# A graph, attention and expert layer on one core: pairs of heads in the order keys, values, queries, with other placements of the products that stand around them

## The reference

```
xn = layernorm(x)                                   # x: 1250 x 1024, 40000 edges (src, dst)
h  = relu(gcn(relu(batchnorm(gcn(xn + pe, W1, b1))), W2, b2))
       # gcn: normalised adjacency (deg**-0.5 on both sides, self loops) times x @ W
q, k, v = xn @ Wq, xn @ Wk, xn @ Wv                 # 16 heads of 64
q_, k_  = relu(q @ proj), relu(k @ proj)            # 256 features a head
attn = (q_ @ (k_.T @ v)) / (q_ @ k_.sum(0) + eps)
x  = x + h + attn @ Wo + bo
x  = x + experts(layernorm(x))                      # top 2 of 8, gated
```

## Time and profile before

| | |
|---|---|
| median of three runs | 1712.08 us (1710.87 to 1712.32) |
| the profiled execution | 1707.89 us |
| its span, first to last instruction | 1705.8 us |
| TensorE matmul busy | 1512.8 us, 89% |
| TensorE weight load busy | 1422.9 us, 83% |
| DVE busy | 803.6 us, 47% |
| ACT busy | 526.4 us, 31% |
| chain that ended last, by engine | PE 76%, DVE 7%, ACT 7%, DMA 5% |
| mean granted TensorE clock | 0.956 of full speed |

### The profile page before, as it was taken

The page is one execution under the profiler, slowest core; times in us unless marked ns, Lnnn a source line. Parts: engine busy times, 40 slices in busy tenths (PEclk is TensorE's granted clock), DMA queues, the critical chain, the costliest instruction groups (busy, mean ns, idle before and its releaser), DMA issues.

```text
span 1705.8 us, 21129 instructions
## 1 busy us (share of the span) xinstructions
PE 1512.8 (89%) x8316; PEld 1422.9 (83%) x8316; DVE 803.6 (47%) x1588; ACT 526.4 (31%) x595; POOL 153.3 (9%) x162
## 2 busy tenths in 40 slices
PE   1689999999999999889899899998997549999996
PEld 1679888989898989789899899998997548998885
DVE  4555565555555564542446333344234455554430
ACT  3324243333334243323222133311111214454441
POOL 0010010101010102000000000000000012222321
PEclk9799999999999999999899999999999559999998
DMA  9531231322121313539344023320442926766763
GB/s 283 181 51 27 39 70 27 73 54 46 51 48 49 51 49 69 208 148 231 101 130 109 13 62 106 100 61 30 114 116 58 304 70 192 199 177 192 188 154 74
DMA packets 72744, 183.62 MB, mean 108 GB/s; under 512 B 8987, under 2 KB 39823, under 8 KB 70927
## 3 DMA queue, kind: packets, MB, share of 16 engines
q1 hardware_dynamic: 52550, 135.17, 25.3%
q0 software_dynamic: 20096, 47.10, 14.9%
HBM read 124.15 MB, written 67.93 MB: 113 GB/s over the span
## 4 chain that ended last, share of the span: by engine, by line
PE 76%; DVE 7%; ACT 7%; DMA 5%; issue 3%; SPq 1%; POOL 0%; POOLq 0%; DVEq 0%; ACTq 0%
PE slot L1441 34%; PE slot L1498 11%; PE slot L1671 6%; PE slot L1681 6%; PE slot L1585 3%; PE kvb L1671 3%; PE kvb L1553 2%; PE slot L1539 2%; DMA raw<-adj_d 2%; PE slot L1576 2%; DMA adj_d<-stage 1%; SPq L500 1%; PE slot L1654 1%; PE lsb L1424 1%; PE lsb L1647 1%
## 5 line engine op out<-in xcount | busy, mean ns | idle before, releaser
L1441 PE MATMUL slot<-big_hi,slab_h 128*128 128x418 f32 x1152 | 294.7, 364 | 26.2 <-issue 8.8
L1441 PE MATMUL slot<-big_lo,slab_h 128*128 128x418 f32 x1152 | 286.6, 357 | 0.0
L1441 PE MATMUL slot<-big_hi,slab_l 128*128 128x418 f32 x1152 | 283.6, 354 | 0.0
L1441 PEld LDWEIGHTS slot<-big_hi,slab_h 128*128 128x128 f32 x1152 | 213.1, 191 | 36.2 <-issue 15.1
L1441 PEld LDWEIGHTS slot<-big_lo,slab_h 128*128 128x128 f32 x1152 | 219.8, 191 | 3.4
L1441 PEld LDWEIGHTS slot<-big_hi,slab_l 128*128 128x128 f32 x1152 | 219.4, 191 | 3.6
L684 POOL DMA_DIRECT2D adj_d<-stage x80 | 67.6, 845 | 585.0 <-ACT stage L752 347.0
L1498 PE MATMUL slot<-adj,xs_h 125*128 125x418 f32 x480 | 118.1, 354 | 0.8 <-DVE ztmp L963 0.5
L1498 PE MATMUL slot<-adj,xs_l 125*128 125x418 f32 x480 | 117.4, 353 | 0.0
L718 POOL DMA_INDIRECT xg<-flat_d,token x32 | 31.3, 977 | 775.2 <-DVE token L1375 657.8
L1498 PEld LDWEIGHTS slot<-adj,xs_h 125*128 125x128 f32 x480 | 90.5, 189 | 2.3 <-DVE ztmp L963 0.7
(11 more groups left out here) (266 smaller groups left out, 2470.8 us busy)
## 6 DMA issues: line engine op xcount, KB each, us to landing
slab_raw<-slabs_dram SPq DMA_DIRECT2D x48, 512.0 KB, 3.8
ws_raw<-w_dram SPq DMA_DIRECT2D x36, 512.0 KB, 5.9
adj_d<-stage POOLq DMA_DIRECT2D x81, 117.2 KB, 3.1
w_raw<-w_dram SPq DMA_DIRECT2D x9, 1024.0 KB, 4.9
adj_d<-eye_dram POOLq DMA_DIRECT2D x1, 6250.0 KB, 26.7
raw<-adj_d SPq DMA_DIRECT2D x3, 1828.8 KB
mix_d<-mixt SPq DMA_DIRECT2D x8, 627.0 KB, 5.0
mix_in<-mix_d SPq DMA_DIRECT2D x8, 627.0 KB, 4.2
```

The costliest lines, as they stand in the source:

```text
L1441: mm = ten.matmul(ps[:, 512 * q:512 * q + CW], w[a][:, kt, :], big[b][:, kt, CW * q:CW * q + CW], start=(kt == 0 and c == 0), stop=(kt == ...
```

## The change

The order of a pair's slabs becomes K, V, Q. The copy of Q's result out of PSUM is a key of its own, `QE`, behind `KK 2`. `KK 0` moves behind the whole Q product, and even `KK` tiles go to `lsb` while odd ones go to the slot whose turn it is, without using up the turn (`places_of`), so Q's slot stays taken until `QE`. `VT` now stands behind `AT p 1` and ahead of `RC` and Q. The ten groups of a pair stand six inside K (behind blocks 2 to 7) and four inside V (behind 3, 4, 6, 7); none is left between the QP products. In `AT p 1` DVE writes `nrm` while ACT writes `num`. In the last pair both heads' QP products come ahead of both AT products, with a second buffer `qp_end`. `RH` moves from behind `KK 5` to behind `KK 6`. At the start, `LN`, `LNS`, `LNB` and `XT` of the tiles are interleaved, `BASE` goes behind the first batch, `WR` behind `XT 7`; the identity copy waits for the first slab. `DG` moves from ahead of `O 5` to ahead of `O 6`; `DT` transposes the degree sums themselves, and their inverse roots are made for each node apart (ACT root, Newton step).

```diff
@@ -54,7 +54,7 @@
-        s += [("K", p), ("Q", p), ("V", p)]
+        s += [("K", p), ("V", p), ("Q", p)]
@@ -68,7 +68,7 @@
-        share[("K", p)], share[("Q", p)] = 6, 4
+        share[("K", p)], share[("V", p)] = 6, 4
@@ -80,7 +80,7 @@
-PARTS = {0: (), 2: (5, 7), 4: (1, 3, 5, 7), 6: (2, 3, 5, 6)}
+PARTS = {0: (), 2: (5, 7), 4: (3, 4, 6, 7), 6: (2, 3, 4, 5, 6, 7)}
@@ -89,39 +89,33 @@
-        inside = WITHIN[key][:4]
-        o += [("EO", g) for g in inside] + [("E", g) for g in inside] + then + [key]
-        return o + [("EO", g) for g in WITHIN[key][4:] if key[0] == "K"]
-
-    o = [("BASE",), ("WR",)]
-    for n, (a, b) in enumerate(LN_TILES):
-        o += [("LN", i) for i in range(a, b)] + [("LNS", n)] + [("LNB", i) for i in range(a, b)]
-        if n:
-            o += [("XT", i) for i in range(*LN_TILES[n - 1])]
-    o += [("XT", NT - 2), ("P", 0), ("XT", NT - 1), ("MP",), ("BASE2",)]
+        return o + [("EO", g) for g in WITHIN[key]] + [("E", g) for g in WITHIN[key]] + then + [key]
+
+    ln = lambda *tiles: [("LN", i) for i in tiles]
+    o = ln(0, 1) + [("LNS", 0), ("BASE",), ("LNB", 0), ("LNB", 1)] + ln(2, 3, 4) + [("LNS", 1), ("LNB", 2)]
+    o += ln(5, 6) + [("XT", 0), ("LNB", 3), ("XT", 1)] + ln(7) + [("LNS", 2), ("LNB", 4), ("XT", 2), ("LNB", 5)]
+    o += ln(8) + [("XT", 3), ("LNB", 6)] + ln(9) + [("LNS", 3), ("LNB", 7), ("XT", 4), ("LNB", 8), ("XT", 5)]
+    o += [("LNB", 9), ("XT", 6), ("XT", 7), ("WR",), ("P", 0), ("XT", 8), ("XT", 9), ("MP",), ("BASE2",)]
...
-        o += ([("KK", p, 0)] if p == 0 else []) + [("KK", p, 1), ("KK", p, 2)]
+        o += [("KK", p, 0), ("KK", p, 1), ("KK", p, 2), ("QE", p)]
         for i in range(3, NT):
             o += [("KV", p, i - 3), ("KK", p, i)]
-            if p and i == 5:
+            if p and i == 6:
                 o.append(("RH", p - 1))
...
-        o += with_split(("K", p + 1)) if more else []
-        behind = WITHIN[("K", p + 1)][4:] if more else []
-        o += [("AT", p, 0), ("QP", p, 1, 0)] + [("EP", g) for g in behind[:1]] + [("E", g) for g in behind[:1]]
-        o += [("QP", p, 1, 1)] + [("EP", g) for g in behind[1:]] + [("E", g) for g in behind[1:]]
-        o += with_split(("Q", p + 1)) if more else []
-        o += [("AT", p, 1), ("RC", p)]
-        o += with_split(("V", p + 1)) + [("KK", p + 1, 0), ("VT", p + 1)] if more else [("RH", p)]
+        if not more:
+            o += [("QP", p, 1, 0), ("QP", p, 1, 1), ("AT", p, 0), ("AT", p, 1), ("RC", p), ("RH", p)]
+            continue
+        o += with_split(("K", p + 1))
+        o += [("AT", p, 0), ("QP", p, 1, 0), ("QP", p, 1, 1)] + with_split(("V", p + 1))
+        o += [("AT", p, 1), ("VT", p + 1), ("RC", p)] + with_split(("Q", p + 1))
     for f in range(KD):
-        if f == 5:
-            o.append(("DG",))
         if f == KD - 1:
             o += [("DT",), ("ZP", 1, 0)]
-        o += with_split(("O", f), {3: [("RP", 0), ("RP", 1)], 4: [("RP", 2)]}.get(f, []))
+        o += with_split(("O", f), {3: [("RP", 0), ("RP", 1)], 4: [("RP", 2)], 6: [("DG",)]}.get(f, []))
...
+def places_of():
+
+    place, before, last, turn = {}, {}, {}, 0
+    for k in ORDER:
+        if k[0] not in PSUM_KINDS:
+            continue
+        if k[0] == "KK":
+            place[k] = (2, turn)[k[2] % 2]
+        else:
+            place[k] = turn
+            turn = 1 - turn
+        before[k] = last.get(place[k])
+        last[place[k]] = k
+    return place, before
...
-            pool.wait_ge(x_landed[NT - 1], LAND)
+            pool.wait_ge(slab_landed[0], 16)
...
-                    copy(chunks(num[o:o + 64, :]), cols(ps)[a:a + 64])
-                    ins = copy(chunks(nrm[o:o + 64, :]), cols(ps)[b:b + 64], bias=ATT_EPS)
-                    ins.then_inc(act_done, 1)
+                    if h == 0:
+                        copy(chunks(nrm[o:o + 64, :]), cols(ps)[b:b + 64], bias=ATT_EPS)
+                    copy(chunks(num[o:o + 64, :]), cols(ps)[a:a + 64]).then_inc(act_done, 1)
...
+                elif kind == "AT":
+                    if k[2] == 1:
+                        dve.wait_ge(psum_full, u)
+                        if k[1]:
+                            dve.wait_ge(att_stored, 32 * k[1])
+                        ts(chunks(nrm[64:128, :]), cols(ps)[0:64], ATT_EPS, ALU.add).then_inc(nrm_made, 1)
...
                 elif kind == "DT":
-                    ten.wait_ge(dve_done, DVED[("DG",)])
+                    ten.wait_ge(deg_ready, 1)
                     for j in range(NT):
-                        mm = ten.transpose(ps[:T, 16 * j:16 * j + 16], dinv_b[0:16, T * j:T * j + T],
+                        mm = ten.transpose(ps[:T, 16 * j:16 * j + 16], ztmp[0][0:16, T * j:T * j + T],
                                            ident[:16, :16])
...
                     if i == 0:
                         ten.wait_ge(dve_done, DVED[("K", p)])
+                        ten.wait_ge(e_copied, WITHIN[("V" if p else "Q", p)][-1] + 1)
+                        if p:
+                            ten.wait_ge(dve_done, DVED[("S", p - 1)])
...
                     if h == 0 and f == 0:
-                        ten.wait_ge(dve_done, DVED[("Q", p)])
+                        ten.wait_ge(dve_done, DVED[("QE", p)])
```

More of the change, by code:

```diff
@@ L170 @@
 DVED = numbered(DVE_KINDS)
-def slot_of(key):
-    return (FULL[key] - 1) % 2
+def places_of():
[11 more added lines that the diff above has]
+    return place, before
+SLOT, BEFORE = places_of()
 RT_ = 105
@@ L320, in build @@
         qp_p = [at(f"qp_{'hl'[q]}", R + 45600 + 10048 * q, [128, 2, NP], F32R) for q in range(2)]
+        qp_end = [at(f"qp_end_{'hl'[q]}", R + 20096 + 10048 * q, [128, 2, NP], F32R) for q in range(2)]
         kk_p = [[at(f"kk_{'hl'[q]}{s}", R + 65696 + 4096 * s + 2048 * q, [T, 2 * FEAT], F32R)
@@ L375, in build @@
         wide = [ps_[:, 0:1024] for ps_ in slot]
+        sums = slot + [lsb]
         group_sum = [lsb[:T, 0:KW], kvb[:T, 0:KW]]
@@ L483, in blocks, with qp @@
             return ps[:rows_, :n * 128].rearrange("p (j c) -> p j c", c=128)[:, :, :w]
+        def qp(q, p, h):
+            return (qp_end if p == PAIRS - 1 and h == 1 else qp_p)[q]
         def v_cols(v):
@@ L755, in _ @@
                 kind = k[0]
-                if kind not in ACT_KINDS and kind not in ("LNS", "WR", "E", "X", "DG", "LN2"):
+                if kind not in ACT_KINDS and kind not in ("LNS", "WR", "E", "X", "DG", "DT", "LN2"):
                     continue
                 if kind in PSUM_KINDS:
-                    u, s = FULL[k], slot_of(k)
-                    ps = slot[s]
-                    if kind not in ("Z", "DG"):
+                    u, s = FULL[k], SLOT[k]
+                    ps = sums[s]
+                    if kind not in ("Z", "DG", "DT"):
                         act.wait_ge(psum_full, u)
+                elif kind == "QE":
+                    ps = sums[SLOT[("Q", k[1])]]
+                    act.wait_ge(psum_full, FULL[("Q", k[1])])
                 if kind == "LNS":
@@ L804, in _ @@
                     act.activation(dinv_b[:, :], ztmp[0][:, :], ACT.Sqrt).then_inc(deg_sqrt, 1)
+                elif kind == "DT":
+                    act.wait_ge(node_degs, 1)
+                    act.activation(nw[:T, NT:2 * NT], nw[:T, 0:NT], ACT.Sqrt).then_inc(node_sqrt, 1)
                 elif kind == "O":
@@ L1065, in _ @@
                 kind = k[0]
-                if kind not in DVE_KINDS and kind not in ("BASE", "LN", "LNS", "WR", "BASE2", "EO", "XC", "XD", "H", "LN2"):
+                if kind not in DVE_KINDS and kind not in ("BASE", "AT", "LN", "LNS", "WR", "BASE2", "EO", "XC", "XD", "H", "LN2"):
                     continue
                 if kind in PSUM_KINDS:
-                    u, s = FULL[k], slot_of(k)
-                    ps = slot[s]
+                    u, s = FULL[k], SLOT[k]
+                    ps = sums[s]
                 if kind == "BASE":
@@ L1188, in _ @@
                        ).then_inc(dve_done, 1)
-                elif kind in ("K", "Q"):
+                elif kind in ("K", "QE"):
                     parts = k_p if kind == "K" else q_p
+                    ps = sums[SLOT[(kind[0], k[1])]]
                     dve.wait_ge(act_done, ACTED[k])
@@ L1401, in free_slot @@
             def free_slot(k):
-                u = FULL[k] - 1
-                if u >= 2:
-                    before = UNITS[u - 2]
+                before = BEFORE[k]
+                if before:
                     if before[0] == "H" and before[1] == 1:
@@ L1409, in free_slot @@
                         ten.wait_ge(deg_ready, 1)
+                    elif before[0] == "Q":
+                        ten.wait_ge(dve_done, DVED[("QE", before[1])])
+                    elif before[0] == "AT" and before[2] == 1:
+                        ten.wait_ge(act_done, ACTED[before])
+                        ten.wait_ge(nrm_made, before[1] + 1)
                     elif before[0] in LAST_READER_DVE:
@@ L1445, in slab_product @@
                         mm.then_inc(psum_full, 1)
```

(6 more changed lines are left out.)

33 lines of the change are left out of this document (19 added, 14 removed).

## The result

The changed kernel takes 1672.11 us, median of four runs (1670.70 to 1674.01), beside 1711.90 (1710.87 to 1712.32) for the kernel before in the same session: ratio 0.9769, with a 95% interval of 0.9752 to 0.9786, some 39.8 us less. Its profiled execution took 1670.70 (span 1669.0), 37.2 less than that of before. The forecast was 1680.7 with a range of 1661 to 1698: right in sign, inside the range, 8.6 too high.

A forecast was written before the change was run, and what follows sets the result against it. TensorE was taken to bound the attention stage nearly throughout. Terms -18 - 3 + 0 + 2.6 - 13 = -31.4, from the median of 1712.1, gave 1680.7; its own range 1669 to 1692, widened by rivals to 1661 to 1698.

The forecast's parts named there:

- Start: Before the pairs: interleaved tiles let ACT and DVE overlap, DVE sets the pace, V 0 starts at 49, not 67.2: minus 18.
- Pair 0: First pair: group waits and a slow-clock wait go, new key-tile waits and restarts come: minus 3 us.
- Pairs: Six pairs after the first: waits that go are replaced by as many others, 0.0 a pair, each between -1.5 and +1.5.
- plus 1.7: K to V in a pair: the QP waits 1.5 for K's copy behind the third transfer, V waits 1.2; 1.7 us more.
- The key tiles' 0.9 and 0.5: Key tiles in a pair: tile 2 waits 0.9 for tile 0's place, tile 5 waits 0.5 behind QE.
- rival B: Pairs lose 2 to 3 each, a transfer taking 4.4 instead of 3.8: 17 in all, 1698; chance 0.14.
- C: Pairs: transfers take 5.0, TensorE waits over 5 before the QP and drops to 1.2 GHz: 37 more, 1718; chance 0.04.
- Rival A: Pairs gain 2 to 3 each, as transfers don't hold K's copy and QE costs nothing: 17 in all, 1663; chance 0.14.
- Last pair: Last pair to O 0: loads from at_d hold O 0, some 11 us idle, slow start; buffer's gain lost: plus 2.6.
- Rival E: At O 0: it is not held by the loads, which move with TensorE: 11 less, 1670; chance 0.04.
- Degrees: Degree sums, O 5 to Z: waits of 5.3 and 3.7 and slow stretches of 1.5 and 2.6 go: minus 13.
- rival F: At the degree sums: DVE's chain holds O 7 or the first Z: +4, 1685; chance 0.55 together with the forecast.

The follow-up runs named there:

- the early loads' run: Changed kernel with SP loading the first six stored pairs from at_d as soon as the last Q product has ended: 1661.31 us, ratio 0.9716 to the kernel before.

## Why the prediction was right, step by step

**Start, forecast -18, measured -18.0, by medians 17.6 when undone.** The walk through the tiles (37 of DVE's work, 6 of stalls, the first tile near 6) gave V 0 at 49, and it is at 49.12. Part of that is luck, since three errors cancel: DVE's first statistics begin at 4.74 (6 was set), DVE is busy for 33.69 (37 was set), and so it is idle for some 10.7 behind its first tile (6 was set). No run takes the new start apart; that DVE sets its pace is argued from where V 0 starts.

**Pair 0, forecast -3, measured -4.8.** The waits that were to go went. The new ones are 0.55, 0.71 and 0.35 at the key tiles, 1.6 where 2.5 was set, and some 1.2 of the gain was not in the step at all: from V 0 to Q 0 only the 1.74 was to go, and 2.9 went (37.8 to 34.9), as TensorE is slow behind V 0 for 3.3 us where it was slow for 6.0. That part is chance, and so is the full clock behind Q 0's wait in this trace. In the four traces that had neither, pair 0 takes 73.4 to 73.7, a gain of 2.2 to 2.5.

**Pairs, forecast 0.0 +- 1.5 each, measured -0.3.** The mechanism was right and one term was mis-sized: the product part's "plus 1.7". I let the sixth group's copy wait for the end of the third transfer's cycle, 18.6 behind K's start (three times 3.8). It waits for the landing only, 3.1 behind the third issue, which is 17.7. So the QP waits 0.47, not 1.5, and V 0.76, not 1.2. V starts 25.6 behind K, not 26.4, and is then set by ACT's chain, as the runs with K's copy first and with the norm on DVE show. The key tiles' 0.9 and 0.5 were 0.72 and 0.35. The other terms came near what was set: beside a pair of before, the good pair from 282.58 gains 1.1 in V's product, loses 0.7 around VT and the wait ahead of Q, and gains 1.5 at the keys (1.2 was set); less the 0.8 by which V starts later than Q did, that is 1.0 in all. Against that stand three pairs of six at 81.5 to 82.6: POOL issued their third transfer 15.3 to 15.9 behind K and not 14.6, and the QP waited 1.2 to 1.9. In the worst, 1.92 brought a slow stretch as well: the QP's 18 matmuls took 5.2 (385.62 to 390.80) and not 3.5. That is rival B's and C's mechanism, in some pairs and not in all. Rival A, a gain of 2.5 in every pair, falls.

**Last pair, forecast +2.6, measured -0.7 up to O 0, and O 0 slow.** The idle of "some 11" was 9.92, ended by the loads, and O 0's first 18 matmuls took 6.30 (711.94 to 718.24) instead of 3.45, so 2.85 lost where 2.6 was forecast. Wrong was the start of O 0: 0.7 earlier and not 1.3 later. The loads went out 78.6 behind K 7 against 77.8 before, 0.8 later, and then took 24.3 instead of 25.9. Rival E, O 0 not held by the loads, falls with the early loads' run. The Trainium skill's rule that long idle gaps drop the clock ("TensorE: Matmul & The Clock Gate", Why this matters for your kernels) agrees with this row: the 2.85 behind 9.92 of idle.

**Degrees, forecast -13, measured -11.9 up to Z (forecast there -11.7), by medians 10.6 when undone.** DG at 797.85 has no wait, and O 6 none. What was named as late next, DVE's chain of 16, ends at 821.7 (805.60 and 16.1), the first ZP at 829.0, and the first Z starts at 832.86: 3.8 to spare, so rival F falls. But the step laid the whole gain to the place of DG and of O 6's split, and the two halves show that the place alone would have given 4.5: with the old roots the long chain is waited for at DT instead of at O 6, 4.28 us with a slow stretch behind it.

**The sum.** The stages made -36.8 where -31.4 was forecast. Of the 5.4 between them, 2.1 are the pairs, 1.8 pair 0, 2.0 O 0's start and 0.2 the degrees, less 0.7 behind the first Z. The other 3 of the 8.6 are the profiled executions: that of before was 4.2 below its median, that of after 1.4.

## What to carry to other kernels

Follow a removed wait to whatever comes in last after it: the second buffer here is worth nothing or 9 us depending on when fourteen loads are issued, and the new place of the degree sums 4.5 or 12.5 depending on what the transposes read. Where an engine's list holds a copy that waits for a transfer, put behind it only what can be as late as that transfer. A wait of TensorE that repeats is to be kept under the lengths that have been seen to bring a slow stretch (here from 1.75 on), since the stretch can cost about as much as the wait (1.6 behind 1.97).

## What the runs showed of the hardware that I had not expected

In the trace of before the clock fell behind waits of 2.37, 3.01 and 3.70, and behind none of the seven of 2.1, so I had priced what is shorter at its length alone. That was too simple, and the same trace held a sign of it: behind a wait of 2.90 in its last pair the 18 matmuls of AT 1 ran at the full clock (granted clock 1.00). The wait of 3.01 at the first AT product of the old last pair, with the lower clock behind it in the trace of before, came back in two runs: in the run with the old last pair the full clock followed, in the one with the early loads besides the lower clock. The wait of 2.90 in the trace of before, and that of 3.01 in these two runs, in this order:

```profile
732.53 0.81 PE L1585 MATMUL slot<-qp_h,s_h 128*128 128x418 f32 x3 [2.90 <-DVE qp_l L1211]
```

```profile
691.91 0.81 PE L1623 MATMUL slot<-qp_h,s_h 128*128 128x418 f32 x3 [3.01 <-DVE s_l L984]
```

```profile
691.94 1.39 PE L1630 MATMUL slot<-qp_h,s_h 128*128 128x418 f32 x3 [3.01 <-DVE s_l L991]
```

Ahead of Q 0, in pair 0, TensorE waits 1.97 in all thirteen traces of changed kernels, always for `kT_l`. In nine of them it goes on at the full clock, in four at the lower one (1.2 GHz), as here at the old start (lower) and in the changed kernel (full):

```profile
104.18 0.96 PE L1479 MATMUL slot<-big_hi,slab_h 128*128 128x418 f32 x3 [1.97 <-DVE kT_l L985]
104.94 1.25 PE L1479 MATMUL slot<-big_lo,slab_h 128*128 128x418 f32 x3
```

```profile
83.98 0.84 PE L1478 MATMUL slot<-big_hi,slab_h 128*128 128x418 f32 x3 [1.97 <-DVE kT_l L984]
84.66 0.74 PE L1478 MATMUL slot<-big_lo,slab_h 128*128 128x418 f32 x3
```

The stretch from Q 0 to K 1 is 36.2 to 36.3 in the nine and 37.8 to 38.0 in the four, and these are the traces with 73.4 to 73.7 for pair 0 in the table. Of the seven waits of 2.0 at key tile 2, with Q's copy early, three were followed by the lower clock, as were waits of 1.75 and 1.82 ahead of a QP in the same run. So behind waits from 1.75 to 3.01 both happen, for 1.97, 2.01 and 3.01 with the same work around them; behind every wait of 3.69 and more between pair 1 and the first Z the clock was low. What decides between them no run here shows. In the four traces in which it fell behind Q 0's wait it had also come back late behind V 0, 5.2 to 6.1 after V 0's start against 3.1 to 3.9 in the nine; yet in the trace of before that was 6.0, and Q 0, behind the same 1.97, ran at the full clock. It may also be a source of the spread from one execution to the next, which is not shown, as each run has one trace: the run with Q's copy early, with many such waits, spread over 14 us (1675.56 to 1689.82), the changed kernel over 3, but the run with the old last pair over 8.
